# Softmax sums of the sixteen-head attention from ones in the value columns, and a division by VectorE alone

## The reference

```
scores = einsum('bhqd,bhkd->bhqk', q, k) / sqrt(16)
attn   = softmax(scores, axis=-1)              # exp(s - max) / sum of exp(s - max)
out    = einsum('bhqk,bhkd->bhqd', attn, v)    # then @ out_w.T + out_b, added to x
```

## Time and profile before

| | |
|---|---|
| median of 3 runs | 1432.4 us (1427.1 to 1432.89) |
| span of the profiled execution | 1426.0 us |
| divisions (lines 1027, 1028) | 48, and 4 in L1 (lines 2153, 2154) |
| mean granted TensorE clock | 0.941 of full speed |

### The profile page before, as it was taken

The page is one execution under the profiler, slowest core; times in us unless marked ns, Lnnn a source line. Parts: engine busy times, 40 slices in busy tenths (PEclk is TensorE's granted clock), DMA queues, the critical chain, the costliest instruction groups (busy, mean ns, idle before and its releaser), DMA issues. The chain is left out here.

```text
span 1426.0 us, 34137 instructions
## 1 busy us (share of the span) xinstructions
PE 1293.6 (91%) x13946; PEld 1054.6 (74%) x13946; DVE 673.4 (47%) x1457; ACT 622.1 (44%) x1444; POOL 429.4 (30%) x549
## 2 busy tenths in 40 slices
PE   4899999976799999999688899999999998859996
PEld 2566666655589999998576678888888887736665
DVE  3676777677322000000654645546446445146666
ACT  2444445521445544444222255545546546135442
POOL 3224446153323222244100143433423423032200
PEclk9999999987799999999666999999999999979998
DMA  9000000000589999996410000000000000000000
GB/s 298 2 2 2 2 2 15 11 17 24 133 291 335 344 344 351 355 352 221 148 32 2 3 1 2 2 1 2 1 2 1 2 2 1 1 1 2 17 17 31
DMA packets 80042, 120.11 MB, mean 84 GB/s; under 512 B 12112, under 2 KB 62544, under 8 KB 79760
## 3 DMA queue, kind: packets, MB, share of 16 engines
q1 hardware_dynamic: 73840, 106.62, 22.4%
q0 software_dynamic: 4768, 10.26, 2.0%
q10 hardware_dynamic: 1280, 1.04, 0.2%
HBM read 108.43 MB, written 9.48 MB: 83 GB/s over the span
## 5 line engine op out<-in xcount | busy, mean ns | idle before, releaser
L1759 ACT ACTIVATE w_ca<-scores,fc1b 128x128 f32<-128x128 f32 x312 | 114.5, 368 | 139.7 <-PE scores L1714 118.6
L912 ACT ACTIVATE reg<-scores 128x1024 f32<-128x1024 f32 x96 | 93.1, 1021 | 160.9 <-PE scores L679 160.7
L1714 PEld LDWEIGHTS scores<-reg 128*128 128x128 f32 x1248 | 146.7, 194 | 6.4 <-issue 2.5
L1714 PE MATMUL scores<-reg 128*128 128x128 f32 x1248 | 147.7, 277 | 3.1 <-issue 1.1
L1724 PE MATMUL bank<-reg,w_ca 128*128 128x256 f32 x624 | 141.1, 379 | 0.3 <-DVE small L1784 0.3
L1006 DVE TENSOR_REDUCE reg<-scores 128x8 f32<-128x1024 f32 x96 | 113.0, 1219 | 54.6 <-PE scores L669 54.5
L2311 ACT ACTIVATE reg<-reg,mx 128x128 f32<-128x128 f32 x256 | 99.1, 389 | 85.1 <-DVE mx L2460 84.8
L2386 POOL TENSOR_TENSOR reg<-reg,rden 128x512 f32<-128x512 f32 x64 | 66.6, 1041 | 212.3 <-DVE rden L2465 212.2
L1793 DVE TENSOR_TENSOR reg<-bank,reg 128x256 f32<-128x256 f32 x39 | 16.6, 425 | 240.9 <-PE bank L1724 232.7
L1724 PEld LDWEIGHTS bank<-reg,w_ca 128*128 128x128 f32 x624 | 115.6, 190 | 14.5 <-DVE small L1784 0.3
L1576 PE MATMUL scores<-reg 128*128 128x128 f32 x1024 | 122.5, 279 | 0.5 <-ACT reg L2327 0.5
(11 more groups left out here) (278 smaller groups left out, 2347.5 us busy)
## 6 DMA issues: line engine op xcount, KB each, us to landing
reg<-in_fc SPq DMA_DIRECT2D x78, 1024.0 KB, 7.4
reg<-expert_out SPq DMA_DIRECT2D x16, 256.0 KB, 3.9
xres<-in_x SPq DMA_DIRECT2D x4, 512.0 KB, 10.6
ctxr<-in_ctx SPq DMA_DIRECT2D x1, 2048.0 KB, 14.8
w_l<-in_w_l SPq DMA_DIRECT2D x2, 1024.0 KB, 12.1
routed_rows<-reg SPq DMA_DIRECT2D x8, 256.0 KB
out<-xres SPq DMA_DIRECT2D x8, 256.0 KB, 2.6
w_sa<-in_w_sa SPq DMA_DIRECT2D x1, 1024.0 KB, 8.5
```

Source lines behind the costliest of these rows:

```text
L912: ins = nc.scalar.activation(PT2[:, t % 2, 2 * half:2 * half + 2, :, :, :].rearrange("p r s c q -> p (r s c q)"), scores4[:, 2 * half:2 * ...
L1714: ins = nc.tensor.matmul(S[n % 4][:, 0:P], up_w8[j % 2][:, c, f * P:(f + 1) * P], xbT[:, j % 2, c, :], start=(c == 0), stop=(c == C - 1))
L1759: nc.scalar.activation(h1[:, j % 2, f, :], S[n % 4][:, 0:P], ACT.Gelu, bias=fc1b[:, bass.ds(e * FC + f, 1)]).then_inc(M["fc1_free"], 1)
```

## The change

- `VP` (and `tok_V`) is filled with ones, not zeros, before the values are written into 16 of each head's 32 columns. So the product of a head leaves 16 rows of values and 16 rows that all hold the head's sum.
- `products` no longer accumulates two heads in one place: even heads go to columns 0 to 255, odd heads to columns 256 to 511, sixteen matmuls of 128 columns, each on its own. The eight matmuls with `ones_half` are gone, and `ones_half` too.
- The division is five DVE instructions, four of them each followed by a wait for its own end (`link`, or `nd_read`): a transpose of the whole bank in 32x32 blocks (512 columns, PSUM to SBUF), a reciprocal of 16 columns of it, a transpose of these, spread over 512 columns, which gives a factor that is 1/sum on the rows of values and zero on the rows of sums, a multiplication of the bank by that factor (512 columns), and an addition of the even to the odd half (256 columns).
- The next `products` waits for `nd_read`, which the multiplication releases, not for `o_ok`, which the addition releases.
- Unused helpers and semaphores are deleted.

```
+        def divided_pairs(dve, link, turned, wide, nd_read, k):
+            link(nc.vector.transpose(turned, banks[4][:, :]))
+            sums_of = turned[:, DH:DH + 2 * (C * P - DH)].rearrange("p (u x) -> p u x", u=2)[:, :, 0:C * P - DH:32]
+            link(nc.vector.reciprocal(den_inv[:, :].rearrange("p (u x) -> p u x", u=2)[:, :, 0:16:2], sums_of))
+            link(nc.vector.transpose(wide.rearrange("p (n u d) -> p n u d", n=16, u=2),
+                                     den_inv[:, 0:32].rearrange("p (n u) -> p n u", u=2).unsqueeze(3).to_broadcast([P, 16, 2, DH])))
+            nc.vector.tensor_tensor(turned, banks[4][:, :], wide, ALU.mult).then_inc(nd_read, 1)
+            dve.wait_ge(nd_read, k)
...
                     def products(b):
-                        for c in range(C):
-                            for s in range(2):
+                        for odd in range(2):
+                            for c in range(C):
                                 for r in range(4):
-                                    nc.tensor.matmul(banks[4][rows_of(r), c * P:(c + 1) * P],
-                                                     VP[:, (b // GB) % 2, b % GB, 8 * c + 2 * r + 1 - s, :],
-                                                     PT2[:, b % 2, r, s, c, :], start=(s == 0), stop=(s == 1))
-                        for s in range(2):
-                            for r in range(4):
-                                ins = nc.tensor.matmul(banks[4][rows_of(r), C * P:2 * C * P], ones_half[:, s, :],
-                                                       PT2[:, b % 2, r, s, :, :], start=(s == 0), stop=(s == 1))
+                                    a0 = (2 * odd + c) * P
+                                    ins = nc.tensor.matmul(banks[4][rows_of(r), a0:a0 + P],
+                                                           VP[:, (b // GB) % 2, b % GB, 8 * c + 2 * r + odd, :],
+                                                           PT2[:, b % 2, r, 1 - odd, c, :], start=True, stop=True)
                         ins.then_inc(M["nd_full"], 1)
...
                             if t - 1 >= 1:
-                                pe.wait_ge(M["o_ok"], t - 1)
+                                pe.wait_ge(M["nd_read"], t - 1)
...
-                            link(nc.vector.reciprocal(rd, banks[4][:, 2 * P:4 * P]))
-                            nc.vector.tensor_tensor(oT_a[:, (b // 2) % 2, :, (b % 2) * P:(b % 2 + 1) * P],
-                                                    banks[4][:, 0:2 * P].rearrange("p (c q) -> p c q", c=C),
-                                                    rd.rearrange("p (c q) -> p c q", c=C), ALU.mult).then_inc(M["o_ok"], 1)
+                            o = oT_a[:, (b // 2) % 2, :, (b % 2) * P:(b % 2 + 1) * P]
+                            if b >= 1:
+                                dve.wait_ge(M["o_ok"], b)
+                            divided_pairs(dve, link, den_turned, den_wide, M["nd_read"], b + 1)
+                            nc.vector.tensor_tensor(o, den_turned[:, 0:2 * P].rearrange("p (c q) -> p c q", c=C),
+                                                    den_turned[:, 2 * P:4 * P].rearrange("p (c q) -> p c q", c=C), ALU.add).then_inc(M["o_ok"], 1)
```

More of the change, by code:

```diff
@@ L331, in store_routed @@
                 .then_inc(ld["xn"], 16)
[L334 to L356, removed]
@@ L358, in pe_turn_rows @@
-        def pe_turn_rows(pe, J, names, src, ok):
-            for c in range(C):
[L361 to L388, removed]
-                bank = claim(pe, J, name)
-                for jj in range(2):
-                    j = 2 * v + jj
-                    for c in range(C):
-                        ins = nc.tensor.matmul(bank[:, jj * D:(jj + 1) * D], src[:, c, j * P:(j + 1) * P],
-                                               w[:, c, w0:w0 + D], start=(c == 0), stop=(c == C - 1))
-                ins.then_inc(q_full[J[name][0]], 1)
@@ L414, in pe_scores @@
-        def pe_scores(pe, j, i):
-            r = slice(64 * (i % 2), 64 * (i % 2) + 64)
-            nc.tensor.matmul(S[i][:, :], qT[r, i // 2, j * P:(j + 1) * P], kM[r, :, i // 2, j * P:(j + 1) * P],
-                             start=True, stop=True).then_inc(M["scored"], 1)
         def bank_of(n):
@@ L475, in pe_turn @@
-        def pe_turn(pe, n):
-            pe.wait_ge(M["scaled"], n + 1)
-            if n >= 2:
-                pe.wait_ge(M["pt_ok"], n - 1)
-            for s in range(4):
-                ins = nc.tensor.transpose(T[n % 2][:, s * P:(s + 1) * P], bank_of(n)[0][:, s, :], ident[:])
-            ins.then_inc(M["turned"], 1)
-        def pe_products(pe, bank, j, out_cols, in_cols, half):
-            for m in range(C):
-                for par in range(2):
-                    for x in range(4):
-                        h = 8 * m + 2 * x + par
-                        ins = nc.tensor.matmul(bank[32 * x:32 * x + 32, m * P + out_cols.start:m * P + out_cols.stop],
-                                               VA[:, j, h, :], PT[:, half, h, in_cols],
-                                               start=(par == 0), stop=(par == 1))
-            return ins
@@ L495, in act_products @@
-        def act_products(act, J, name, bv, dst_cols):
-            bank = await_full(act, J, name)
-            for c in range(C):
-                ins = nc.scalar.activation(oT[:, c, dst_cols], bank[:, c * P:(c + 1) * P], ACT.Identity, bias=col(bv, c))
-            ins.then_inc(q_free[J[name][0]], 1)
         class Home:
@@ L1439, in build @@
         tok_bias = out_bias[:, 0, :]
+        tok_turned, tok_wide = [junk[:, 4 * k:4 * k + 4, :].rearrange("p k n -> p (k n)") for k in range(2)]
         KV = ["hc0", "hc1", "k0", "k1", "v0", "v1"]
```

110 lines of the change are left out of this document (21 added, 89 removed).

## The result

The changed kernel takes 1424.0 us (median of 16 runs, 1419.57 to 1430.89), the kernel before 1431.93 us in 16 runs beside them (1427.1 to 1437.78). The ratio is 0.9946, with a 95% interval from 0.9931 to 0.9961: faster by 7.9 us, where I had forecast 19 to 20. The profiled execution has a span of 1421.0 us, that of before 1426.0 us.

The account below looks back on a forecast made before the run. PE was taken to bound the attention slots, with the score loop and POOL's chain close behind. Terms of 23.8 us less 4 us for the clock gave a span of 1406.2 us, plus 6.4 about 1413 us; range 1403 to 1427 us.

Parts of the forecast that it names:

- the forecast: Whole kernel, main case: a gain of 12 to 25 us, 1407 to 1420 us, at 1413 us; chance 0.66.
- PE's slots: Thirteen long or middle slots in L0 and L3: each loses the sums' 0.97 us, 12.6 us in all.
- the eight short ones: Short slots of L0 and L3: 0.42 us less each, down to the score loop's 6.96 us, 3.4 us together.
- DVE's division: DVE, per batch: 2.71 us of instructions, 2.80 with waits, against 2.18 before, so 0.62 us more.
- The step-zero rival: Second transpose on DVE reads slowly, taking 1.05 to 1.4 us: 1423 to 1431 us; chance 0.06.
- a rival with 0.10: Dear transposes on DVE: gain gone at 1.1 us each, 1445 us at 1.36, 1600 us at 3.5; chance 0.10.
- The three hold-ups in POOL's chain: L0's cross stage: maxima queue behind POOL's normalisation once a group; first gains 0.2 us, the other two -0.4 us together.
- the clock as 1 us: Lower clock after PE idles: 1 us for three hold-ups, 0.4 us for four L3-end waits; 4 us total, between 0 and 12.
- The router's slots t=23 to 26: L0 slots with router work in PE's order: a gain of 3.4 us.
- L0's end: After t=26 DVE sets the pace and divides back to back: -0.6 us, between -2 and +1.
- L1 and L3's end: L1's chain gains 3.9 us (6.0 less 2.1); L3's last two batches gain 1.3 us (1.94 less 0.62).
- The clock eats it: Rival: new idle stretches end at 1.2 GHz, three hold-ups and L3's end, taking about 16 us: 1424 us; chance 0.10.

Follow-up runs that it names:

- the run without the sums: Kernel before without the eight matmuls of sums in L0's and L3's products, old division reading the products instead (output wrong): 1417.1 us (0.986).
- the run with the fill: Changed kernel plus 18, 10, 10 and 8 idle PE matmuls ahead of scores_turned at t=10, 14, 18, 23: 1424.85 us (0.9936).
- two buffers: Also "both buffers": changed kernel with two buffers each for mv and the router's row statistics: 1405.7 us (0.9784), second run 1407.0 us (0.9819).

## Why the prediction came out as it did

The direction was right; the size was not: 7.9 us, not 19 to 20, and below the 12 to 25 us of the forecast. That 1424.0 us still lies in the wide range (1403 to 1427) is in part luck: the span came out at 1421.0 us, 14.8 above the 1406.2 of the sum, but the median lay only 3.0 us above that span, where I had added 6.4.

*PE's slots: right, 0.11 us too much in each.* In the first profiles all thirteen slots that I had given to PE and the eight short ones got shorter, the short ones to 6.96 us as forecast. PE's slots got 0.86 us shorter, not 0.97: in the kernel before the next matmuls, those of the sums, started 0.90 us after products (201.65 to 202.55 in the timeline), now the projection starts 1.01 us after them (196.01 to 197.02).

```profile
201.65 1.08 PE L689 MATMUL bank<-reg 128*32 128x128 f32 x32
```

In the run without the sums, where the products are the old ones, it is 1.01 us too, so it is what follows that makes the difference, and not the new products; I counted the hold of the removed group alone. Thirteen times 0.11 is 1.4 us.

*DVE's division: right, a little short.* 2.81 us of instructions against 2.71, the transposes 0.71 against 0.68 us; with the waits 2.95 against 2.80, so DVE got about 0.73 us more per batch, not 0.62. The step-zero rival is out: the transpose that reads each column sixteen times took 711 ns, as the dense one. The Trainium skill ("Vector Engine (DVE) Microarchitecture Reference", § 3.8) says that the transpose is pipelined to one element per cycle and lane; the trace agrees, with 711 ns beside 691 ns for a multiplication of the same 512 columns. I had left this out and kept an upper bound of 3.5 us, and a rival with 0.10, that this sentence speaks against.

*The three hold-ups in POOL's chain: mechanism right, sum short by 3.4 us.* From POOL's start to scores_turned it was 16.17 us (185.71 to 201.88), 16.11 forecast, and PE's waits were 2.87 to 4.78 us, 2 to 4.7 forecast. What was mis-sized is what follows a wait: I booked the clock as 1 us for each of the three and as 4 us for all of L0 and L3 together (the terms named there already make 4.6). By the run with the fill it was 2.48 us at t=10, nothing at t=14, 1.52 at t=18 and 1.85 at t=23, 5.85 us in all, beside more at t=25 and at the end of L3.

*The router's slots t=23 to 26: wrong, the step that failed.* I gave them 3.4 us, "four times 0.97, less 0.5", without following who waits there as I had done for the three groups. They lost 4.6 us, 8 us off: against the forecast of each slot 4.2 us at t=23, 1.0 at t=24 and 3.3 at t=25, less the 0.5. POOL's chain of the last group ends (biases at line 771, to 238.06) and only then POOL centres the router's first rows (to 241.68); the router's second statistics wait for that, and the maxima for these. That is the fourth hold-up: 11.03 us for t=23, and 6.96 with two buffers. At t=24 the slot gains nothing (8.08 us before, 8.06 after): where the sums stood, PE now waits 0.89 us for DVE to move the output rows (line 842). At t=25 it is the lower clock: 13.53 us before, 15.86 after, 14.3 with the fill, and 12.67 in the second run with both buffers, where the clock stayed up. The rows of this slot, before, after and in that run:

```profile
259.61:273.14 13.53, 12.42 (x151) 8.58 (x150) 6.57 (x14) 6.40 (x10) 3.35 (x4) 1.00 0.06 21
258.16:274.02 15.86, 14.75 (x136) 10.67 (x135) 9.09 (x23) 7.70 (x11) 3.35 (x4) 0.78 0.05 18
239.92:252.59 12.67, 11.56 (x135) 8.11 (x134) 7.68 (x19) 6.41 (x10) 3.34 (x4) 1.00 0.06 22
```

Even with both buffers these four slots gained 1.0 to 2.1 us, not 3.4.

*L0's end: not shown to be wrong.* The two profiles of one kernel differ there by more than the forecast.

*L1 and L3's end: 2.5 to 6.5 us too much.* The sums of L1 went as forecast, but its gain was 1.1 to 2.7 us, and none where L1 took 111.9 us. At L3's end the two groups of sums were paid back by the longer wait for the division and by scores_turned and products at the lower clock.

*The rivals.* "The clock eats it" named 1424 us, the time that came, by coincidence. It is not what happened: it put 6 us into the hold-ups, which fits, but 8 us into L3's end, which came out 1.3 to 3.7 us below its forecast, and with the clock kept up in the hold-ups the kernel was no faster. The larger part is the wait in the queue: taking the waits away gave 17 to 18 us by the medians. The rival that stood behind this case but was not written down is that the thing beside PE with nothing to spare appears four times, not three.

## What to carry to other kernels

When an engine gets faster, walk through every place where its successor's work stands in an in-order queue behind a wait for a third engine, and through each stage, also those that look irregular: here two sets of statistics with one buffer each turned 22 to 24 us into 8. The cure is not at the engine that was sped up: a second copy of 16 and of 20 columns per partition, or the step that releases the third engine moved ahead of a long one. And two or three profiles of the unchanged kernel tell which differences of stages mean anything.

## What the runs showed of the hardware

The granted clock of TensorE did not follow the length of an idle stretch alone. After a wait of 2.86 us at t=14 scores_turned ran at full speed in both profiles of the changed kernel, after one of 2.87 or 2.86 us at t=18 it ran at 1.2 GHz, 1.92 or 1.85 us instead of 1.17. L1, the same program in both, took 106.35 us in the changed kernel (twice the same to 0.1 us) and 111.92 us in the version with both buffers (twice), at a mean granted clock of 0.70 and 0.64:

```profile
705.95:812.30 106.35, 87.16 (x1764) 74.26 (x1764) 61.09 (x186) 21.86 (x35) 6.62 (x16) 0.70 0.04 12
```

```profile
686.03:797.95 111.92, 92.50 (x1763) 79.35 (x1763) 61.17 (x186) 21.86 (x35) 6.61 (x16) 0.64 0.04 11
```

In the two profiles of the kernel before it took 109.0 and 107.4 us. Both profiles with the two buffers are of the slowest execution of their series (1411.8 us of 1401.6 to 1411.8, and 1410.3 of 1406.1 to 1410.3), so these runs do not settle whether the edits in L0 or the single execution moved the clock of L1; it is 5.6 us, most of what the change itself gained.
